# Paged attention: the new keys of four heads handled in row tiles, and turned copies moved ahead of exponentials

## What is computed

```python
L = NPP * PSIZE                                  # 16 pages of 32 keys = 512 cached keys
kc = k_cache[block_table].reshape(bsz, L, HK, D) # HK = 8 key heads, D = 128
vc = v_cache[block_table].reshape(bsz, L, HK, D)
k_all = jnp.concatenate([kc, k], axis=1)         # + the 32 new keys: 544
v_all = jnp.concatenate([vc, v], axis=1)
valid_c = jnp.arange(L)[None, :] < cache_seqlens[:, None]
valid = jnp.concatenate([valid_c, jnp.ones((bsz, seqlen), dtype=bool)], axis=1)
scores = jnp.einsum('bqhd,bkhd->bhqk', q, k_all) * SCALE     # 32 query heads, 4 per key head
scores = jnp.where(valid[:, None, None, :], scores, -1e+30)
probs = jax.nn.softmax(scores, axis=-1)
o = jnp.einsum('bhqk,bkhd->bqhd', probs, v_all)
```

## Time and profile before

| | us |
|---|---|
| median of 3 runs | 1833.53 (1832.86 to 1836.39) |
| profiled execution | 1838.09 |
| its span in the trace | 1836.3 |
| TensorE busy in the span | 1694.5 (92%) |
| VectorE busy | 1117.0 (61%) |
| ScalarE busy | 990.6 (54%) |
| mean rate of the DMA engines | 158 GB/s |

### The profile page before, as it was taken

One profiled execution on the slowest core, in us unless ns is written; L12 is line 12 of the kernel. 1 busy time (PEld: TensorE's weight loads), 2 busy tenths in 40 slices (PEclk: granted clock), 3 DMA queues, 4 the chain that ended last, 5 costly groups with the idle time before them and its releaser, 6 DMA issues. The chain is left out here.

```text
span 1836.3 us, 35368 instructions
## 1 busy us (share of the span) xinstructions
PE 1694.5 (92%) x10952; PEld 1460.9 (80%) x10952; DVE 1117.0 (61%) x2883; ACT 990.6 (54%) x2485; POOL 461.7 (25%) x388
## 2 busy tenths in 40 slices
PE   2895999999998899999959999999999999989999
PEld 2884777777776788888758999999999999867775
DVE  8304432544335567777758888888888888734442
ACT  3223223222222257666659888888988888722220
POOL 1012121221211146655412222232222322221210
PEclk9997999999999999999979999999999999989999
DMA  7521011101110333444487888778887888275511
GB/s 237 179 104 63 1 63 63 63 3 60 63 58 24 129 115 110 127 130 127 137 283 257 271 282 268 259 259 276 279 267 254 265 277 282 100 211 163 141 37 46
DMA packets 232476, 290.64 MB, mean 158 GB/s; under 512 B 19018, under 2 KB 175082, under 8 KB 232426
## 3 DMA queue, kind: packets, MB, share of 16 engines
q1 hardware_dynamic: 213994, 222.89, 38.0%
q0 software_dynamic: 18432, 67.12, 10.5%
HBM read 237.43 MB, written 50.41 MB: 157 GB/s over the span
## 5 line engine op out<-in xcount | busy, mean ns | idle before, releaser
L1446 PE MATMUL p_val<-probs_t,vals 128*128 128x128 f32 x2560 | 328.5, 276 | 0.0
L1446 PEld LDWEIGHTS p_val<-probs_t,vals 128*128 128x128 f32 x2560 | 306.8, 192 | 0.0
L1381 DVE CUSTOM_DVE_ANT_0 probs<-p_score,mask 128x544 f32<-128x544 f32 x256 | 184.5, 721 | 64.2 <-issue 64.2
L1312 ACT ACTIVATE probs<-probs,low 128x544 f32<-128x544 f32 x256 | 191.0, 746 | 34.5 <-DVE low L1381 23.3
L1431 PE MATMUL p_turn<-cst,probs 128*128 128x128 f32 x1024 | 157.4, 276 | 29.0 <-ACT probs_t L1320 23.2
L1369 DVE TENSOR_TENSOR wo_lo<-keys,wo_hi 128x544 fp32r<-128x544 f32 x256 | 183.6, 717 | 0.0
L1307 ACT ACTIVATE wo_hi<-keys 128x544 fp32r<-128x544 f32 x256 | 166.5, 651 | 29.8 <-PE p_score L1423 28.1
L1320 ACT ACTIVATE probs_t<-p_turn 128x640 f32<-128x640 f32 x256 | 175.2, 685 | 1.0 <-PE p_turn L1432 1.0
L450 PE MATMUL p_tile<-w_hi,y_hi 128*128 128x512 f32 x384 | 159.1, 414 | 4.6 <-PEq L463 2.4
L1431 PEld LDWEIGHTS p_turn<-cst,probs 128*128 128x128 f32 x1024 | 112.7, 140 | 52.9 <-issue 48.4
L452 PE MATMUL p_tile<-w_hi,y_lo 128*128 128x512 f32 x384 | 152.4, 397 | 0.0
(11 more groups left out here) (207 smaller groups left out, 3927.7 us busy)
## 6 DMA issues: line engine op xcount, KB each, us to landing
keys<-in_k_pages SPq DMA_DIRECT2D x512, 128.0 KB, 2.9
qk_new<-stage SPq DMA_DIRECT2D x80, 256.0 KB, 2.3
x_res<-qk_new SPq DMA_DIRECT2D x32, 512.0 KB, 3.7
o_new<-x_res SPq DMA_DIRECT2D x32, 512.0 KB
w_raw<-in_w_vkq_t SPq DMA_DIRECT2D x12, 1024.0 KB, 5.5
w_raw<-in_w_qkv_t SPq DMA_DIRECT2D x10, 1024.0 KB, 8.3
toep<-kpad SPq DMA_DIRECT2D x32, 256.0 KB, 4.6
w_raw<-in_w_dense_t SPq DMA_DIRECT2D x8, 1024.0 KB, 5.4
```

What stands on the lines that cost most here:

```text
L1312: nc.scalar.activation(probs[:, i % 4, :], probs[:, i % 4, :], ACT.Exp, bias=low[:, i % 4:i % 4 + 1], scale=-1.0, accum_out=total[:, i % 4 ...
L1381: v.tensor_tensor_reduce(out=probs[:, i % 4, :], in0=p_score[:, i % 2, FROM:FROM + KEYS], in1=mask[:, i // HK, :], scale=1.0, scalar=3e38, ...
L1446: mm = pe.matmul(p_val[:, i % 2, 0:P], vals[:, slot, n, cols], probs_t[:, i % 2, n, :], start=(n == 0), stop=(n == 4))
```

## The change

- **Order of the new keys.** Scores of odd steps have the 32 new keys ahead of the 512 cached ones, those of even steps behind them. So the new keys are loaded twice, in front of and behind the pages. Scores of an even and an odd step lie side by side in three banks (`FROM`), of which both use the middle one. The fourth score product therefore waits until the step before is masked.
- **Probabilities** of two steps lie side by side, in four double buffers, so the new keys of an even and an odd step are 64 neighbouring columns.
- **Transposes.** Four for each step. Behind those of each fourth step two products with the identity turn the 64 new columns of two steps each, into partitions 0 to 63 and 64 to 127 of unused columns of the first value bank.
- **Values.** Four products for each step, one bank for each of four steps. Behind the fourth step come four products with 32 rows each, one for each step, for the new keys.
- **Copies.** The turned copy has 512 columns instead of 640, with one of 128 in every fourth step (`take_turned_new`). The output copy is one of 4 x 128 in every fourth step instead of 128 in each, and the next four steps' values wait for it.
- **Order on ScalarE.** `take_turned(i-4)` is done before `exponent(i-2)`.
- **Around it.** The zeros above the new values and the memset that made them go; the new values are loaded as 4 x 32 rows; the constants have 32 more columns; the page numbers are bounded in `make_rows` and no longer one by one on SyncE.

The core of the diff:

```diff
-        vals = sb("vals", [P, 2, NPP // 4 + 1, HK * D])
+        vals = sb("vals", [P, 2, NPP // 4, HK * D])
+        vals_new = sb("vals_new", [P, 2, HK // NEW, D])
...
+        p_score = ctx.enter_context(nc.psum_tensor("p4_score", [P, 3 * E], F32))
+        p_turn = ctx.enter_context(nc.psum_tensor("p4_turn", [P, 4, P], F32))
+        p_val = ctx.enter_context(nc.psum_tensor("p4_val", [P, NEW, E], F32))
...
+        HAS = (slice(1, NPP + 2), slice(0, NPP + 1))
+        ENDS = (slice(0, LONG), slice(SHORT, KEYS))
+        MIDDLES = (slice(LONG, KEYS), slice(0, SHORT))
+        FROM = (E - LONG, E + KEYS - LONG)
+        score_at = lambda n, part: p_score[:, FROM[n] + part.start:FROM[n] + part.stop]
+        probs_of = lambda i: probs[:, i // 2 % 4, i % 2 * KEYS:(i % 2 + 1) * KEYS]
...
-                    sp.dma_start(keys[slot][:, NPP, :, :].rearrange("p h s -> p (h s)"), mine[:, 0:KW]).then_inc(done, 16)
+                    sp.dma_start(keys[slot][:, 0:NPP + 2:NPP + 1, :, :].rearrange("p n h s -> p n (h s)"), bc(mine[:, 0:KW], 1, [P, 2, KW])).then_inc(done, 16)
...
+                    new = v_new[bass.ds(row, S), :].rearrange("t (q h d) -> h t q d", h=NEW, d=D)
+                    sp.dma_start(vals_new[:, slot, :, :].rearrange("p q d -> p (q d)"), new).then_inc(v_new_in[slot], 16)
...
-                nc.scalar.activation(probs_t[:, i % 2, :, :], p_turn[:, 0:5, :], ACT.Copy).then_inc(turned_taken, 1)
-
-            def take_values(m, i):
-                r = m * RB + i
-                slot, k = i // HK, i % HK
-                act.wait_ge(val_done, r + 1)
-                if k == 0 and not (isinstance(m, int) and m == 0):
+                nc.scalar.activation(probs_t[:, i % 2, :, :], p_turn[:, :, :], ACT.Copy).then_inc(turned_taken, 1)
+
+            def take_turned_new(m, q):
+                n = m * QUADS + q
+                act.wait_ge(new_turned, n + 1)
+                if not (isinstance(n, int) and n < 2):
+                    act.wait_ge(new_done, n - 1)
+                nc.scalar.activation(probs_nt[:, q % 2, :], p_val[:, 0, P:2 * P], ACT.Copy).then_inc(new_taken, 1)
+
+            def take_values(m, q):
+                n, slot, half = m * QUADS + q, q // 2, q % 2
+                act.wait_ge(new_done, n + 1)
+                if half == 0 and not (isinstance(m, int) and m == 0):
                     act.wait_ge(out_stored[slot], 32 * m)
-                nc.scalar.activation(outs[:, slot, k * P:(k + 1) * P], p_val[:, i % 2, 0:P], ACT.Copy).then_inc(out_ready, 1)
+                nc.scalar.activation(half_heads(outs, slot, half).rearrange("p (h n) -> p h n", h=NEW), p_val[:, :, 0:P],
+                                     ACT.Copy).then_inc(out_ready, 1)
+
+            def late(m, i):
+                take_turned(m, i)
+                if i % NEW == NEW - 1:
+                    take_turned_new(m, i // NEW)
+
+            def later(m, i):
+                if i % NEW == NEW - 1:
+                    take_values(m, i // NEW)
 
             def body(m, first):
                 for i in range(RB):
                     split_hi(m, i)
+                    step_of(m, i - 4, first, late)
                     step_of(m, i - 2, first, exponent)
-                    step_of(m, i - 4, first, take_turned)
-                    step_of(m, i - 5, first, take_values)
+                    step_of(m, i - 5, first, later)
...
-                if not (isinstance(r, int) and r < 4):
-                    v.wait_ge(turned, r - 3)
+                if i % NEW == 0 and not (isinstance(r, int) and r < 8):
+                    v.wait_ge(new_turned, m * QUADS + i // NEW - 1)
                 v.memset(wait_carrier[:, i % 4:i % 4 + 1], 0.0)
-                v.tensor_tensor_reduce(out=probs[:, i % 4, :], in0=p_score[:, i % 2, FROM:FROM + KEYS], in1=mask[:, i // HK, :],
+                v.tensor_tensor_reduce(out=probs_of(i), in0=score_at(i % 2, slice(0, KEYS)), in1=mask[:, i // HK, S - i % 2 * S:S - i % 2 * S + KEYS],
...
-                a, b = slice(0, A_KEYS), slice(A_KEYS, KEYS)
-                to_a, to_b = p_score[:, i % 2, FROM:E], p_score[:, i % 2, E:FROM + KEYS]
+                end, middle = ENDS[i % 2], MIDDLES[i % 2]
                 hi, lo = q_hi[:, slot, k * P:(k + 1) * P], q_lo[:, slot, k * P:(k + 1) * P]
-                pe.matmul(to_a, hi, k_hi[:, i % 2, a], start=True, stop=False)
-                pe.matmul(to_b, hi, k_hi[:, i % 2, b], start=True, stop=False)
-                pe.matmul(to_a, hi, k_lo[:, i % 2, a], start=False, stop=False)
-                pe.matmul(to_b, hi, k_lo[:, i % 2, b], start=False, stop=False)
-                pe.matmul(to_a, lo, k_hi[:, i % 2, a], start=False, stop=True)
-                pe.matmul(to_b, lo, k_hi[:, i % 2, b], start=False, stop=True).then_inc(scores_done, 1)
+                three_pass(pe, score_at(i % 2, end), hi, lo, k_hi[:, i % 2, end], k_lo[:, i % 2, end], True, True)
+
+                if not (isinstance(r, int) and r < 1):
+                    pe.wait_ge(masked, r)
+                three_pass(pe, score_at(i % 2, middle), hi, lo, k_hi[:, i % 2, middle], k_lo[:, i % 2, middle], True,
+                           True).then_inc(scores_done, 1)
 
             def transposes(m, i):
                 r = m * RB + i
...
                 if not (isinstance(r, int) and r < 1):
                     pe.wait_ge(turned_taken, r)
                 for n in range(4):
-                    pe.transpose(p_turn[:, n, :], probs[:, i % 4, n * P:(n + 1) * P], ident)
-                pe.transpose(p_turn[:, 4, :], probs[:, i % 4, KEYS - P:KEYS], ident).then_inc(turned, 1)
+                    at = i % 2 * S + n * P
+                    mm = pe.transpose(p_turn[:, n, :], probs_of(i)[:, at:at + P], ident)
+                mm.then_inc(turned, 1)
+                if i % NEW == NEW - 1:
+
+                    for a in range(2):
+                        mm = pe.matmul(p_val[2 * a * S:2 * (a + 1) * S, 0, P:2 * P], probs[:, (i // 2 - 1 + a) % 4, CACHE:CACHE + 2 * S], ident,
+                                       start=False, stop=True, skip_group_check=True)
+                    mm.then_inc(new_turned, 1)
 
             def values(m, i):
                 r = m * RB + i
-                slot, k = i // HK, i % HK
+                slot, k, q, h = i // HK, i % HK, i // NEW, i % NEW
+                n = m * QUADS + q
                 if k == 0:
                     pe.wait_ge(vals_gathered[slot], VALS * m + VALS)
                     pe.wait_ge(v_new_in[slot], 16 * m + 16)
-                    pe.wait_ge(rows_cleared, 1)
                 pe.wait_ge(turned_taken, r + 1)
-                if not (isinstance(r, int) and r < 2):
-                    pe.wait_ge(out_ready, r - 1)
-                cols = slice(k * D, (k + 1) * D)
-                for n in range(5):
-                    mm = pe.matmul(p_val[:, i % 2, 0:P], vals[:, slot, n, cols], probs_t[:, i % 2, n, :], start=(n == 0), stop=(n == 4))
+                if h == 0 and not (isinstance(n, int) and n < 1):
+                    pe.wait_ge(out_ready, n)
+                for c in range(4):
+                    mm = pe.matmul(p_val[:, h, 0:P], vals[:, slot, c, k * D:(k + 1) * D], probs_t[:, i % 2, c, :],
+                                   start=(c == 0), stop=False, skip_group_check=True)
                 mm.then_inc(val_done, 1)
+                if h == NEW - 1:
+                    pe.wait_ge(new_taken, n + 1)
+                    for a in range(NEW):
+                        at = slice(a * S, (a + 1) * S)
+                        mm = pe.matmul(p_val[:, a, 0:P], vals_new[at, slot, q % 2, :], probs_nt[at, q % 2, :], start=False, stop=True, skip_group_check=True)
+                    mm.then_inc(new_done, 1)
```

62 lines of the change are left out of this document (31 added, 31 removed).

## The result

| | median | lowest to highest | runs |
|---|---|---|---|
| before | 1833.19 us | 1832.56 to 1836.39 | 4 |
| after | 1789.55 us | 1788.74 to 1792.52 | 4 |

The changed kernel takes 0.9761 of the time, with a 95% interval of 0.9745 to 0.9778: 43.6 us less. The prediction was 1779.5 (1758 to 1812). The range held, but the middle was 10 us too good. The small miss hides half of the story: of the two parts of the change, one brings everything and the other nothing.

What follows compares the result with a forecast made beforehand. TensorE's work plus a wait for the turned copy bounds attention: four heads 10.40 to 9.55 us, 62 groups give 52.7; with 1.8 and -0.5 it is 54. From 1838.1, less 4.6 for the median: 1779.5 us, range 1758 to 1812.

Steps and rivals of the forecast that it cites:

- What bounds the kernel: Attention stage: TensorE's 2.42 us per head plus 0.18 waiting for the turned copy, held behind mask and exponential by order alone.
- turned copies ahead of exponentials: ScalarE's order in the attention stage: the wait before the transposes goes, gaining 0.18 us per head, to 2.42.
- Part 2, work: Packing new keys: one transpose and one value product fewer per head; TensorE's work 2.10 us, added products 0.21 and 0.27.
- Part 2, edges: TensorE's changes of tile form around both added blocks: 0.1 us per edge, 0.4 in four heads; skill-based estimate 0.7.
- rival of dear blocks: Added TensorE blocks have full-drain edges or no concurrency: up to 10.07 us for four heads, 1785 to 1812 us; chance 0.15.
- Part 3a: First value product of the next four heads waits for the 128x512 output copy: 0.25 us in four heads, 0.06 per head.
- slower than before: Late ScalarE holds up the single set of value banks; decides from 1.1 us wait in four heads; 1857 us at 1.5; chance 0.05.
- Part 3b: Fourth score product waits for the previous head's mask in the middle of p_score: 0.5 us of slack, taken as 0.
- 3c: Copy of the turned new keys is wanted a value block later, 0.83 us against 0.3: no wait.
- the other engines: All keep up with 2.39 us per head: VectorE 2.11, ScalarE 2.07, DMA engines 2.16 at a share of 0.91.
- The ends: Start and end of the attention stage: memset gone, -1.8 us; one more block and a longer last copy, +0.5 us.
- the first eight heads gain nothing: Start of the attention stage: the second batch's keys come at the DMA queue's pace, so only 248 heads gain.

Runs made afterwards that it cites:

- order_again: The kernel before with one edit: ScalarE's copy out of the turn bank stands ahead of the exponential; 1792.1 us, ratio 0.9760.
- double_blocks: The changed kernel with the 64-column pair and the four 32-row products issued twice, so new keys count twice; 1810.7 us, ratio 0.9871.
- after_again: The whole changed kernel, unedited, measured a second time beside the kernel before; 1793.2 us, ratio 0.9772.
- out_first: The changed kernel with ScalarE's copy of the four value banks moved ahead of the exponential; 1783.6 us, ratio 0.9728.
- full_turn: The changed kernel with the 64-column pair replaced by two full transposes, copied out apart; ratio 0.9602 on the first chip, 1783.0 us when repeated on another.

## Why the prediction was right, and where its sizes were off

- **What bounds the kernel: right.** The chain is one of order alone. The part "turned copies ahead of exponentials" was put at 0.18 per head, to 2.42, and order_again has 2.42 in every step of the steady stretch.
- **Part 2, work: right.** 2.10 per head was predicted, 2.08 measured. That four 32-row products run side by side was read from the 0.063 us in the earlier trace rows; 0.22 for the four is what double_blocks shows, against 0.27 (and 0.21 against 0.22 for the pair).
- **Part 2, edges: the term that was mis-sized.** The prediction took 0.1 us for an edge from the one gap ahead of a block in the earlier trace rows, and as much for its end: 0.4 for four edges. They measured 0.35 + 0.39 = 0.74 (double_blocks). The row gave the edge into a block ahead of 32-column tiles; the edge out was only assumed, and four heads have two blocks with both. By the rule of the Trainium skill's "TensorEngine Tiling (Array Packing)", section "Key Properties", with the drain from its "TensorE: Matmul & The Clock Gate", section "Single matmul latency", the prediction had also worked out an estimate of 0.7, and the runs agree with it. The row was given the greater weight, and wrongly.
- **So the outcome lies in the rival of dear blocks** (1785 to 1812, given 0.15), just outside the forecast's own 1770 to 1785, and by that rival's mechanism. The range held because it took that rival in. What the prediction had not seen is how little this leaves: the packing was to gain 10.40 - 4 x 0.18 - 9.55 = 0.13 in four heads, and edges of 0.74 take that away. The sum of the change was off by a fifth (54 against 43.6), and the share of its second part was wrong altogether: 0.13 x 62 = 8 us were put there. order_again is 1 us faster than after_again, where the runs of the two spread over 4 and 7 us, and in steps 16 to 240 the packing brings 0.3 to 0.7 us where 0.13 x 56 = 7 were put.
- **Part 3a, the value banks: right in place, 0.15 instead of 0.25.** With the dearer 32-row block TensorE comes 0.14 later to the same copy, so less of the wait is left. out_first shows it to be this copy. The rival "slower than before" wanted a wait of 1.1.
- **Part 3b, 3c, the other engines: right.** No wait for the middle of p_score, none for the turned new keys; a DMA share of 0.90 against 0.91; VectorE 453 and ScalarE 443 of 500.
- **The ends: half right.** The start lost the memset's 1.8 us and another 1.8; how they divide by cause was not tried. (The 512-KB load of the second batch's queries was also issued 3.7 us after the first one instead of 7.25.) But "the first eight heads gain nothing" was too kind: everything starts earlier against the same DMA engines, and the second batch's keys are waited for 5.62 instead of 1.47. Start and first 16 steps gave 1.3 where 3.5 were expected. The last 16 steps gave 1.1 where 3.4 were in the sum: in both kernels they hold the step in which VectorE stands beside GpSimd's subtraction (6.27 us before, 7.46 after). What follows them gave 1.4 where 0.5 of loss was expected.
- **The sum.** 52.7 us were predicted for 62 groups at 0.85. The measured 0.70 or 0.71 over the 56 groups of steps 16 to 240 makes 39.6 instead of 47.6, 8 of the 10 us that are missing; the ends are the rest.

Open: what releases ScalarE late on the chip of the first group, and why the kernel before loses 87 us there (its mean granted clock is 0.960 to 0.965 there and 0.975 to 0.979 on the other chips; no trace of it was taken); and how the 43.6 us would divide on that chip, where full_turn, although it takes work from TensorE, was slower (0.960) than the order alone (0.952). No experiment was made on that. Why the key pages land later in the packed kernel (a median of 4.4 us from issue to landing in after_again, 2.9 in order_again) was not tried either; no wait in the steady stretch ends in them.

## What to carry to other kernels

Before packing small products into tiles, count how often TensorE changes its mode, and price each change from a trace. Here it was 0.17 to 0.2 us: a block of one full product's length needed some 0.35 us of saved products beyond its own length before it gained anything, and a full-width product that computes twice what is needed can be cheaper than a tile that does not. Change the order of instructions first: when an engine waits for a copy that stands behind unrelated work in another engine's queue, one moved line may bring all of the gain, and the two parts of a change should be timed alone before the larger one is credited. And where the DMA engines are full, a stall that is taken away comes back with the next load.

## What the runs showed of the hardware

- A change of TensorE's tile form cost 0.17 to 0.20 us per edge beside the products, in fp32 at a granted clock of 1.00; two products of 64 columns or four of 32 rows take 0.22 us together, as long as one full one (double_blocks, full_turn_again).
- A wait at a TensorE product is read from the weight loads: at the value banks the starts of the products put 0.07 us of it ahead of the value products and 0.07 into them, the starts of the weight loads put all 0.15 ahead (after against out_first).
- A stall of TensorE of 4 us cost more than itself: the granted clock fell to 0.80 and 0.63 in the stretches around it, and the step behind it took 3.20 us instead of 2.08 (after).
- GpSimd's 128x2048 subtraction of 4.5 us stretched a VectorE instruction of 0.50 us to 5.33, though VectorE's recorded start was 0.49 us earlier; VectorE ended 0.30 to 0.32 us behind GpSimd in six traces.
- One chip ran the kernel before 4.8% longer than the others did (1920.8 against 1833 to 1834 us), and the changed orders at 1818 to 1868: there the kernels differ in another proportion than elsewhere.
